# Head of a two-layer kernel: query weights split on GpSimd, and another order of the first three units

## The reference

```python
xn = _layernorm(x, axis=-1)                       # x is 8 x 1024 x 256
qkv = xn @ W; q, k, v = split(qkv)                # W is 256 x 768
q = elu(q) + 1; k = elu(k) + 1
KV = einsum('bld,blh->bhd', k, v); k_sum = k.sum(axis=1)
s = einsum('bld,bhd,bl->blh', q, KV, 1 / (einsum('bld,bd->bl', q, k_sum) + EPS))
logits = einsum('th,eh->te', xn, gate_w)          # 8 experts, the best one is taken
g = silu(expert(xn))
x = x + s * g
```

## Time and profile before

| | us |
|---|---|
| median of 3 runs (lowest to highest) | 522.12 (520.51 to 523.44) |
| the profiled execution, its own time | 517.94 |
| its span | 516.2 |
| TensorE busy | 499.0 |
| VectorE busy | 456.9 |
| ScalarE busy | 393.1 |
| GpSimd busy | 307.5 |

### The profile page before, as it was taken

The page is one execution under the profiler, slowest core; times in us unless marked ns, Lnnn a source line. Parts: engine busy times, 40 slices in busy tenths (PEclk is TensorE's granted clock), DMA queues, the critical chain, the costliest instruction groups (busy, mean ns, idle before and its releaser), DMA issues.

```text
span 516.2 us, 12184 instructions
## 1 busy us (share of the span) xinstructions
PE 499.0 (97%) x3576; PEld 461.1 (89%) x3576; DVE 456.9 (89%) x1420; ACT 393.1 (76%) x891; POOL 307.5 (60%) x367
## 2 busy tenths in 40 slices
PE   6899999999999999899999999999999999999995
PEld 5899999999999999799999988878888888888884
DVE  6899999999999987669988948989999999999985
ACT  4878878787878774567777856878888887888883
POOL 5568866777676877332222038887777787785200
PEclk9999999999999999999999999999999999999999
DMA  8942322222222115457778664266666555655311
GB/s 228 243 118 88 123 84 81 84 83 83 83 84 83 43 62 193 135 164 237 224 229 262 197 196 124 89 131 139 132 139 137 123 135 131 142 134 111 83 42 62
DMA packets 59415, 67.83 MB, mean 131 GB/s; under 512 B 11864, under 2 KB 53728, under 8 KB 59360
## 3 DMA queue, kind: packets, MB, share of 16 engines
q1 hardware_dynamic: 44416, 38.82, 24.7%
q0 software_dynamic: 14944, 28.32, 22.7%
HBM read 39.85 MB, written 27.26 MB: 130 GB/s over the span
## 4 chain that ended last, share of the span: by engine, by line
PE 78%; DVE 6%; SPq 6%; issue 3%; DMA 3%; ACT 1%; POOL 1%; POOLq 0%; DVEq 0%
PE v_ps L1464 9%; PE q_ps L1442 9%; PE s_ps L1484 5%; PE k_ps L168 3%; PE gu_ps L1123 3%; PE k_ps L169 3%; PE m_ps L168 3%; PE k_ps L170 3%; PE m_ps L170 3%; PE m_ps L169 3%; PE tq_ps L168 3%; PE tq_ps L169 3%; PE tq_ps L170 3%; PE tq_ps L400 3%; PE pa_ps L1495 3%
## 5 line engine op out<-in xcount | busy, mean ns | idle before, releaser
L1816 POOL DMA_INDIRECT four<-expert_rows,gather_u x64 | 69.5, 1086 | 38.1 <-DMA expert_rows<-y 19.5
L949 POOL DMA_INDIRECT sorted_rows<-xn,row_u x64 | 68.0, 1063 | 17.2 <-issue 13.9
L938 POOL TENSOR_TENSOR xn<-xn 128x512 fp32r<-128x512 f32 x32 | 43.2, 1350 | 30.7 <-ACT xn L563 30.4
L1464 PE MATMUL v_ps<-wvo,xt 128*128 128x256 f32 x256 | 60.6, 379 | 0.0
L1442 PE MATMUL q_ps<-xt,wqk 128*128 128x256 f32 x256 | 60.6, 379 | 0.0
L1579 ACT ACTIVATE xn2nd<-res,shift,rstd 128x256 f32<-128x256 f32 (+1 forms) x64 | 34.9, 593 | 26.7 <-DVE shift L1686 26.6
L1442 PEld LDWEIGHTS q_ps<-xt,wqk 128*128 128x128 f32 x256 | 48.5, 190 | 6.9 <-issue 0.4
L209 POOL DMA_DIRECT2D four<-sorted_rows x36 | 19.7, 548 | 56.6 <-issue 53.4
L1464 PEld LDWEIGHTS v_ps<-wvo,xt 128*128 128x128 f32 x256 | 46.3, 190 | 5.0
L1822 POOL DMA_DIRECT2D res<-in_L_attn_x x26 | 35.1, 1391 | 17.6 <-DVE res L1642 16.0
L1831 POOL TENSOR_TENSOR rstd<-var_eps,neg_half 128x4 f32<-128x4 f32 x32 | 36.6, 1143 | 11.9 <-DVE var_eps L1678 11.8
(11 more groups left out here) (260 smaller groups left out, 1748.1 us busy)
## 6 DMA issues: line engine op xcount, KB each, us to landing
expert_rows<-y SPq DMA_DIRECT2D x36, 256.0 KB, 3.1
four<-in_L_attn_x SPq DMA_DIRECT2D x32, 256.0 KB, 2.9
out_rows<-att SPq DMA_DIRECT2D x32, 256.0 KB, 2.1
res<-in_L_attn_x POOLq DMA_DIRECT2D x26, 256.0 KB, 4.9
four<-sorted_rows SPq DMA_DIRECT2D x36, 128.0 KB, 2.6
four<-sorted_rows POOLq DMA_DIRECT2D x36, 128.0 KB, 2.8
wdn<-in_L_ffn_wd SPq DMA_DIRECT2D x2, 512.0 KB, 7.4
sorted_rows<-res SPq DMA_DIRECT2D x8, 128.0 KB, 5.8
```

Of the source, the lines that this page charges most:

```text
L938: nc.gpsimd.tensor_tensor(xn2[:, s, 1], xn[:, i], xn2[:, s, 0].bitcast(F32), ALU.subtract).then_inc(g["xn_split"], 1)
L949: nc.gpsimd.indirect_dma_start(out=z.sorted_dram.ap(), out_offset=bass.IndirectOffsetOnAxis(ap=row_u[:, i // CU, k:k + 1], axis=0), in_=xn ...
L1464: m = nc.tensor.matmul(v_ps[:, t, :], xt[:, i % 2, k, t * P:(t + 1) * P], wvo[:, k, :], start=(t == 0 and k == 0), stop=(k == KD - 1), ski ...
L1816: nc.gpsimd.indirect_dma_start(out=moe[:, n % SLOTS, t, :], out_offset=None, in_=z.expert_dram.ap(), in_offset=bass.IndirectOffsetOnAxis(a ...
```

## The change

The query weights' rest (`wq`, second part) is subtracted by GpSimd behind its casts, with a semaphore of its own, `wq_split`. The gate's weights are loaded behind the first two parts of W, centred behind the first part and turned behind turn(0). The v part is loaded behind x of unit 2, spread on TensorE behind keys(0), centred in unit 1 behind the routing, and rounded and split in units 3 and 4. TensorE takes q(1) ahead of turn(2). ScalarE takes exp q(0) ahead of the rounding of turned unit 1, applies the norm of unit 3 ahead of exp q(1), and rounds xn(0) behind exp keys(0). VectorE takes the statistics of unit 1 ahead of the split of turned unit 0 (as before), with the call moved.

```diff
@@ sync @@
-                    if part == 0:
+                    if part == 1:
                         sp.dma_start(gate_s[:], gate_w).then_inc(g["gate_loaded"], 16)
...
-                if isinstance(m, int) and m in (0, 1):
+                if isinstance(m, int) and m in (0, 2):
                     load_weights((0, 1) if m == 0 else (2,))
...
-                    sp.wait_ge(g["split"], 4)
+                    sp.wait_ge(g["wq_split"], 1)
+                    sp.wait_ge(g["split"], 3)
@@ tensor @@
-                        pe.wait_ge(g["split"], 4)
+                        pe.wait_ge(g["split"], 3)
...
                 if begin:
-                    stay_warm(2)
-                    spread_end(2)
-                    pe.wait_ge(g["split"], 1)
+                    pe.wait_ge(g["gate_centred"], 1)
+                    for k in range(KD):
+                        t = nc.tensor.transpose(gate_ps[:, k], gate_c[:, k * P:(k + 1) * P], z.ident[0:E, 0:E])
+                    t.then_inc(g["gate_turned"], 1)
+                    stay_warm(4)
+                    pe.wait_ge(g["wq_split"], 1)
+                if n <= 1:
                     q(n, i, r)
                 turn(n + 1, at(i, 1))
-                if not begin:
+                if n > 1:
                     q(n, i, r)
                 if begin:
-                    pe.wait_ge(g["split"], 3)
+                    pe.wait_ge(g["split"], 2)
                     pe.wait_ge(g["cast"], 5)
                 keys(n, i, r)
+                if begin:
+                    spread_end(2)
@@ scalar @@
-                begin = isinstance(n, int) and n <= 0
                 round_sums(n, i, r)
-                if begin and n == -2:
+                if n == -2:
                     norm_apply(0, 0)
                     round_weights((0,))
+                if n == 0:
+                    exp_q(n, i)
                 round_turned(n + 1, at(i, 1))
-                if begin:
+                if n == -1:
+                    round_weights((1, 2))
+                if -1 <= n <= 1:
+                    norm_apply(n + 2, at(i, 2))
+                if n == 0:
+                    exp_keys(n, i)
+                if n == 1:
                     exp_q(n, i)
-                if begin and n == -1:
-                    round_weights((1, 2))
-                if begin and n > -2:
-                    norm_apply(n + 2, at(i, 2))
                 round_xn(n, i)
                 rows(value_of(n - 1))
-                if not begin:
+                if n > 1:
                     exp_q(n, i)
-                if not begin:
                     norm_apply(n + 2, at(i, 2))
-                exp_keys(n, i)
+                if n != 0:
+                    exp_keys(n, i)
                 round_kv(n, i, r)
                 round_next(value_of(n + 1))
-                if begin and n == 0:
+                if n == 3:
                     round_weights((3,))
@@ vector @@
-                if begin and n == -2:
+                if n == -2:
+                    centre_weights(0)
                     centre_gate()
-                    centre_weights(0)
                     centre_weights(1)
-                    split_weights((0,))
-                if begin and n == 0:
-                    centre_weights(2)
+                if n == 0:
                     fill_q(n, i)
...
-                split_turned(n + 1, at(i, 1))
-                if begin and n == -1:
+                if n != -1:
+                    split_turned(n + 1, at(i, 1))
+                if n == -1:
                     split_weights((1, 2))
...
+                if n == -2:
+                    split_turned(0, 0)
...
+                if n == 1:
+                    centre_weights(2)
                 if n == 2:
                     sum_columns()
+                if n == 4:
                     split_weights((3,))
@@ gpsimd @@
+                    dst, src = weights[0]
+                    pool.wait_ge(g["rounded"], 1)
+                    nc.gpsimd.tensor_tensor(dst[:, 1], src, dst[:, 0].bitcast(F32), ALU.subtract).then_inc(g["wq_split"], 1)
```

More of the change, by code:

```diff
@@ L280, in first_layer @@
         count_ps = k_ps[:, 0, NK:NK + (CT + 1) * E]
-        g = sems("gate_loaded moe_w_loaded selector ends_spread blank consts cast gate_centred gate_turned part_centred centred rounded split step "
+        g = sems("gate_loaded moe_w_loaded selector ends_spread blank consts cast gate_centred gate_turned part_centred centred rounded wq_split split step "
                  "zeroed zeros_stored "
@@ L527, in tensor @@
             spread_end(0)
[L528 to L531, removed]
             spread_end(1)
@@ L870, in step @@
                 ahead = n + 3, at(i, 3)
-                begin = isinstance(n, int) and n <= 1
-                if begin and n == -2:
+                if n == -2:
+                    centre_weights(0)
                     centre_gate()
-                    centre_weights(0)
                     centre_weights(1)
-                    split_weights((0,))
-                if begin and n == 0:
-                    centre_weights(2)
+                if n == 0:
                     fill_q(n, i)
@@ L890, in step @@
                 stats_complete(*ahead)
-                if not (begin and n == 0):
+                if n != 0:
                     fill_q(n, i)
```

## The result

The changed kernel took 524.06 us in the median of 19 runs (522.00 to 527.06), the kernel before 520.32 us in 19 runs beside it (518.95 to 523.71). The ratio of their times is 1.0067, with a 95% interval of 1.0048 to 1.0085: 3.5 us slower, between 2.5 and 4.4. The forecast was 3.4 us over the kernel before. It was given as 525.5 us, from the median of three runs (522.12 us) that lay 1.8 us above the median of the nineteen.

The account below looks back on a forecast made before the run. TensorE's unbroken first-layer stream was taken as the bound, closing up at sums(1), released by VectorE. Delays of 2.5 + 0.9 = +3.4 us on the 522.12 us median gave 525.5 us, range 521.0 to 527.8.

Parts of the forecast that it names:

- Step 1: Head: GpSimd's `wq` split blocks VectorE's second last-row step, delaying unit 1's statistics from 8.87 to 9.24: +0.4 us.
- The rival that VectorE wins the tie: Head: VectorE's last-row step starts before GpSimd's `wq` split; head 1.1 us shorter, total +2.3, 524.4 us; chance 0.15.
- Step 2: TensorE's new order before sums(1): turn(3) at about 20.4 against 21.28, a 0.9 us lead depending on the next step.
- Step 3: Unit 1: longer line to fill q(1), added centring and blocked VectorE operations put sums(1) at 27.2 against 24.68: +2.5 us.
- Step 4: End of unit 4: the moved wv split and meetings with GpSimd delay the first row's kv: +0.9 us (+0.3 to +1.2).
- Step 5: SP's queue: x of unit 9, behind the later `gu_end` loads, lands by 47.7, wanted at about 49: costs nothing.
- if that cover is gone: SP's queue: without the over 1 us in hand for x of unit 9, the load costs what it is late.
- The clock: Rival: clock falls in longer idle stretches before q(0) and sums(1): +5 to +8, about 528 us; chance 0.05.

Follow-up runs that it names:

- e5: Changed kernel with the two `gu_end` loads issued four units later, behind x(12); 521.76 us, ratio 1.0049 to the kernel before.
- e7: Kernel before with only the `wq` split moved to GpSimd; 519.51 us, ratio 0.9998 to the kernel before.
- e10: Changed kernel with an added wait: GpSimd splits `wq` only after VectorE's second last-row step; 521.52 us, ratio 1.0058.
- e8: Changed kernel with `wq` split on VectorE, exp q(1) ahead of unit 3's norm, value centring behind unit 1's key split, wv handled in unit 2; 517.67 us, ratio 0.9975.
- e2: Changed kernel with the centring of the value columns moved ahead of fill_q(1) in unit 1; 520.02 us, ratio 1.0037.
- e3: Changed kernel with ScalarE's exp q(1) put back ahead of the norm of unit 3; 520.97 us, ratio 1.0049.
- e1: Changed kernel with the `wq` split given back to VectorE; 521.07 us, ratio 1.0070 to the kernel before.
- e11: Changed kernel with six throw-away matmuls ahead of sums(1), none added before q(0); 522.76 us, ratio 1.0075.
- e4: Changed kernel with wv rounded and split in unit 2 again, as before the change; 522.61 us, ratio 1.0096.
- e12: The changed kernel run once more, unedited; 522.37 us, ratio 1.0073 to the kernel before.
- e6: Changed kernel with throw-away matmuls in both idle stretches: 10 instead of 4 before q(0), 6 new before sums(1); 522.01 us, ratio 1.0047.
- e9: e8 with the value centring ahead of fill_keys(1) instead of behind unit 1's key split; 518.30 us, ratio 0.9991.

## Why the prediction was right, and where not

**Step 1 (+0.4): right.** The step of 0.35 us took 1.26, 1.38 and 0.91 us in three executions of the changed order, since GpSimd began 0.04 to 0.5 us ahead in each. Statistics at 9.27 in e5 against 9.24 forecast, and +0.4 us alone in e7. The rival that VectorE wins the tie came in none of the profiles; forced by e10, the other order is worth 0.7 us at sums(1), not the 1.1 that I gave it, for 0.3 us goes to neg_mean. The key columns did not land sooner in this profile (spread at 6.70, before 6.54), though they did in others (6.20 in e8): landing varies by more than the issue that it was moved.

**Step 2 (TensorE 0.9 ahead at turn(3)): right.** 20.29 in e5, 20.4 forecast. In the changed kernel's own profile it is 21.79, since the clock fell from 13 to 16.5 us.

**Step 3 (+2.5): right, term by term.** In e5 sums(1) is at 27.07, +2.39. e2 takes away the centring (0.6) and the blocked key split (1.0) and gives 1.5; e3 takes away the long line to fill_q(1) with the blocked neg_mean and gives 1.46. With e1's 0.5 that is 3.5, and e8, which has all three, starts sums(1) 3.63 us before e5: they add up. (The head was earlier by chance, by 0.2 us in e8 and 0.1 in e3; without that it is 3.4 on both sides.)

**Step 4 (+0.9): wrong.** Two things failed in it. "Now VectorE has 0.6 us more in front of it" overlooked that VectorE idles just there. The kernel before, then e5:

```profile
37.81 0.69 DVE L716 TENSOR_TENSOR k<-kf,k 128x512 fp32r<-128x512 f32 x1 [0.61 <-ACT k L591]
```

```profile
39.51 0.68 DVE L812 TENSOR_TENSOR wv<-w_s,wv 128x512 fp32r<-128x512 f32 x1
40.20 0.69 DVE L722 TENSOR_TENSOR k<-kf,k 128x512 fp32r<-128x512 f32 x1
...
40.41 1.07 POOL L940 TENSOR_TENSOR rstd<-var_eps,neg_half 128x2 f32<-128x2 f32 x1
```

The key split of unit 4 waited 0.61 us for ScalarE; the split of wv fills that gap, and the split of the sums ends 0.4 us before kv starts in both (39.10 and 39.52 before, 41.49 and 41.90 in e5). And "meet GpSimd's `rstd` and scatter work (0.4 and 0.5 ...)" charged the waiting to the wrong engine: VectorE's splits keep their length while the scatter (39.39, 0.99 us) runs, and it is `rstd` that becomes longer, 1.07 us against 0.70. It does so in the kernel before too (38.02, 1.07 us), so that it isn't a cost of the change at all.

**Step 5 (nothing): wrong, mis-sized.** "With 2.9 us to land, or twice that" was 7.5 us (issued at 43.96 and in e11 at 41.89, statistics at 51.49 and 49.41) and 8.0 in e2 (39.98, 47.94): x(9) was issued 0.8 to 1.1 us behind the second of two loads of 256 KB for `gu_end`, which themselves took up to 8 us. Without them in front, two loads of x issued between 37 and 44 us landed in 2.5 and 2.7 us (e5); 1.9 us behind them, x(9) landed in 4.4 (before, issued at 30.78). It costs 1.0 us where the clock holds (e11 against e5), less where a fall has already held TensorE up. I had named this as what it costs "if that cover is gone". All these loads are of 256 KB; I should have bounded the landing by the row of x(9) itself and those of `gu_end` in the trace of before (4.4, 4.9 and 5.7 us), not by the median of six loads. And "VectorE wants it at about 49" was late by almost 2 us: in e11 it idles for x(9) from 47.3 on, and in e5 it takes these statistics at 47.11. So there was no cover of 1 us, and even 5.8 us to land would have been 0.4 us too long.

**The sum.** 2.4 for steps 1 to 3, 0 for step 4, 1.0 for step 5: 3.4 us, the forecast's figure, since the two errors of 0.9 and 1.0 cancel. The first 2.4 us were forecast by their mechanism; that the total fits too is luck.

**The clock, given 0.05: too little.** It comes on top of steps 1 to 3, and a fall behind sums(1) in place of the wait for x(9). The price was wrong too: no fall here cost the 5 to 8 us that I gave. Of the seven profiles with 1.81 to 1.84 us of idling before sums(1) (the changed kernel, e1, e3, e4, e5, e10, e12), five show a fall between 24 and 34 us; of the seven with 0.51 us or less there (before, e2, e6 to e9, e11), none does. Each costs 1.4 to 1.5 us on the spot. These counts tie the fall to the idling; e6 and e11, which fill it with matmuls, are only two profiles. A second place is before q(0): the changed kernel, e7 and e9, with 1.96, 2.38 and 1.93 us of idling, show one between 11.5 and 16.5 us, while before with 2.10 and four others with 1.97 to 2.07 don't; of six with 1.52 or less none does. (In three of the six, e6, e11 and e12, there is so little idling because the matmuls ahead of it ran at nearly half pace: 8 of them took 2.08 us in e11 and 1.99 in e12, against 1.16 in e5, though the granted clock of that stretch reads 1.00. The cause is open.) My argument, "No row here shows a fall after 2.10", took one execution for all. In the median the falls behind sums(1) are worth less than they look, as e11 beside e12 shows, because they overlap with the wait for x(9). The profiled execution had two falls in the head, and that is why it is 5.80 us late at the end of the layer. A third, near 224 us (0.96 from 200 to 240 us), shows in seven of the fourteen profiles and not in that of before. Its cause was not tried: before idles 1.62 us at that place, the changed kernel 1.61. The rest of the 9.2 us of span, between 207.76 and the end, holds that fall and was not taken apart further.

## What to carry to other kernels

Moving an operation from VectorE to GpSimd relieves VectorE only if it doesn't meet an SBUF operation there: look at who begins first, to 0.1 us, and if need be add a wait so that the short operation goes first (e10 gained 0.7 us at sums(1) by a wait, too little to show in its time). Place new work on an engine where its own rows show idle time, not just ahead of a step that another engine waits for. When a load is put behind a wait in a queue, price the transfer behind it by what is now just ahead of it; and when an edit leaves TensorE idle for as long as here (1.8 to 2.4 us), profile it several times, since the clock fell in some executions only.

## What the runs showed of the hardware beyond the forecast

- The granted clock fell to its lower level in some executions and not in others of the same order: e5 and e12 idle 1.84 and 1.83 us before sums(1), and only e12 falls, near 28 us. Where it did fall there, a dozen or so matmuls ran at 0.38 to 0.42 us in place of 0.28, and it cost 1.4 to 1.5 us.
- A VectorE operation of 128x2 elements was held up for 0.75 us (neg_mean, 0.92 in place of 0.17) and one of 128x256 for 1.0 us (1.38 in place of 0.35) by one GpSimd instruction of 1.27 us; a lead of 0.04 us was enough (7.93 against 7.97).
- A 256 KB load that landed 2.5 to 2.7 us from issue with none just ahead of it (e5) took 7.5 to 7.9 us issued 0.8 to 1.1 us behind two other loads of 256 KB each (e11, e2), and 4.4 us issued 1.9 us behind them (before).
